# Two graph layers on one core: where the row sums of the attention weights are summed and inverted

## The reference

```
h = relu(layernorm(x))
q, k, v = h Wq' + bq, h Wk' + bk, h Wv' + bv
weight = adj * exp(q k')                     # 256 x 256 per graph
weight = weight / sum(weight, over the keys)
x = x + weight v                             # layer 0
h = relu(layernorm(x))
deg = sum(adj, over j);  agg = (adj h) / max(deg, 1e-6)
x = x + relu([h, agg] W1')                   # layer 1
```

## Time and profile before

| | before |
|---|---|
| median of 3 runs | 2078.81 us (2077.85 to 2078.81) |
| span of the profiled execution, first to last instruction | 2075.8 us |
| what lies around the span (median less span) | 3.0 us |
| TensorE busy | 2033.4 us, 98% |
| VectorE busy | 1420.9 us, 68% |
| GpSimd busy | 1015.8 us, 49% |
| ScalarE busy | 772.6 us, 37% |

### The profile page before, as it was taken

One profiled execution on the slowest core, in us unless ns is written; L12 is line 12 of the kernel. 1 busy time (PEld: TensorE's weight loads), 2 busy tenths in 40 slices (PEclk: granted clock), 3 DMA queues, 4 the chain that ended last, 5 costly groups with the idle time before them and its releaser, 6 DMA issues.

```text
span 2075.8 us, 28517 instructions
## 1 busy us (share of the span) xinstructions
PE 2033.4 (98%) x9852; PEld 1702.4 (82%) x9852; DVE 1420.9 (68%) x2329; ACT 772.6 (37%) x1289; POOL 1015.8 (49%) x958
## 2 busy tenths in 40 slices
PE   8899999999999999999999999999999999999999
PEld 5688888888888888888888888888888888888887
DVE  6877676776667776767767677766677676767654
ACT  3433434333343334343333433344433334333432
POOL 3555553554544555535555445455355554454520
PEclk9999999999999999999999999999999999999999
DMA  5121122212222221222122221212221222212101
GB/s 188 61 76 67 66 76 91 81 51 76 72 85 81 70 72 66 76 91 81 51 72 75 86 81 65 76 66 76 91 81 51 71 76 86 81 60 82 63 29 51
DMA packets 114753, 155.30 MB, mean 75 GB/s; under 512 B 10800, under 2 KB 75312, under 8 KB 114736
## 3 DMA queue, kind: packets, MB, share of 16 engines
q1 hardware_dynamic: 114736, 155.08, 22.0%
HBM read 121.38 MB, written 33.68 MB: 75 GB/s over the span
## 4 chain that ended last, share of the span: by engine, by line
PE 87%; DVE 10%; issue 1%; DMA 0%; SPq 0%; ACT 0%; DVEq 0%; ACTq 0%
PE bank L337 28%; PE bank L339 28%; PE bank L338 28%; DVE hT_l L689 4%; PE bank L345 3%; DVE y L800 1%; DVE x L815 1%; DVE sums L834 1%; DVE h L831 1%; DVE h L730 0%; DMA x_in<-x 0%; DVE sum_inv L836 0%; DVE w_l L175 0%; DVE w L745 0%; DVE v_l L684 0%
## 5 line engine op out<-in xcount | busy, mean ns | idle before, releaser
L292 POOL TENSOR_TENSOR xT<-xT,shared 128x512 f32<-128x512 f32 x248 | 455.5, 1874 | 162.0 <-DMA shared<-norms 162.0
L325 POOL TENSOR_TENSOR at_l<-adjT,at_h 128x1024 fp32r<-128x1024 f32 x32 | 81.4, 2545 | 308.4 <-ACT at_h L675 308.4
L337 PE MATMUL bank<-hT_h,n_h 128*128 128x512 f32 x512 | 204.0, 399 | 23.6 <-DVE x L815 23.1
L269 POOL TENSOR_TENSOR rs<-var_eps,minus_half 128x2 f32<-128x2 f32 x128 | 89.7, 701 | 272.4 <-DVE var_eps L706 272.4
L730 DVE CUSTOM_DVE_ANT_0 h<-h,u_b,bqk 128x512 f32<-128x512 f32 x128 | 215.0, 1731 | 0.0
L535 ACT ACTIVATE h<-x,rs 128x512 f32<-128x512 f32 x124 | 94.1, 807 | 313.5 <-POOL rs L275 313.5
L579 ACT ACTIVATE y<-bank 128x512 f32<-128x512 f32 x128 | 76.7, 599 | 355.6 <-PE bank L339 355.6
L175 POOL TENSOR_TENSOR w_l<-w,w_h 128x512 fp32r<-128x512 f32 x62 | 80.4, 1297 | 255.1 <-ACT w_h L597 255.1
L338 PE MATMUL bank<-hT_l,n_h 128*128 128x512 f32 x512 | 200.3, 391 | 0.0
L339 PE MATMUL bank<-hT_h,n_l 128*128 128x512 f32 x512 | 200.1, 391 | 0.0
L337 PE MATMUL bank<-wv_h,hT_h 128*128 128x512 f32 x512 | 199.2, 389 | 0.0
(11 more groups left out here) (125 smaller groups left out, 4865.9 us busy)
## 6 DMA issues: line engine op xcount, KB each, us to landing
x_in<-x SPq DMA_DIRECT2D x32, 1024.0 KB, 5.3
xT<-x_t SPq DMA_DIRECT2D x62, 512.0 KB, 6.6
out<-x SPq DMA_DIRECT2D x124, 256.0 KB, 2.0
adjT<-adj_t SPq DMA_DIRECT2D x32, 512.0 KB, 3.5
shared<-adj SPq DMA_DIRECT2D x32, 512.0 KB, 4.8
shared<-norms SPq DMA_DIRECT2D x31, 512.0 KB, 3.6
x<-wq SPq DMA_DIRECT2D x4, 256.0 KB, 3.8
xb<-wk SPq DMA_DIRECT2D x4, 256.0 KB, 4.4
```

Source lines behind the costliest of these rows:

```text
L269: pool.tensor_tensor(rs[n][:, 0, tiles], var_eps[n][:, tiles], minus_half[:, :], ALU.pow).then_inc(rstd_done[n], 1)
L292: pool.tensor_tensor(tile, tile, norms[:, k * T:(k + 1) * T, :], (ALU.mult, ALU.add)[k]).then_inc((xT_scaled, xT_shifted)[k], 1)
L325: pool.tensor_tensor(at_l[:, :, :], adjT[:, :, :], at_h[:, :, :].bitcast(F32), ALU.subtract).then_inc(at_split, 1)
L337: pe.matmul(dst, lh, rh, start=first, stop=False)
```

## The change

For a step that has a layer 1 and a following pair (steps 1 to 30), TensorE issues `sums()` after `layer1_products(1)`, and VectorE runs `sum_inverses()` after `layer1_result(1)` and `low_hT(1)`. In step 0 and step 31 both stay where they were. No instruction is added or dropped.

```
--- before.py
+++ after.py
@@ -500,8 +500,10 @@
                 if layer1 and more:
                     for t in range(T):
                         layer1_products(t)
-                if layer0:
-                    if layer1:
+                        if t == 1:
+                            sums()
+                if layer0:
+                    if layer1 and not more:
                         sums()
                     for t in range(T):
                         av(t)
@@ -891,11 +893,14 @@
                     for t in range(T):
                         layer1_result(t)
                         low_hT(i + 1, t)
+                        if t == 1:
+                            sum_inverses()
                 if layer0:
                     if not layer1:
                         for t in range(T - 1):
                             low_hT(1, t)
-                    sum_inverses()
+                    if not (layer1 and more):
+                        sum_inverses()
                     if not layer1:
                         low_hT(1, T - 1)
                     layer0_result(0)
```

## The result

The changed kernel takes 2045.02 us (median of 4 runs, 2044.71 to 2046.76) against 2078.6 us before (a fourth run has joined the three behind 2078.81): a ratio of 0.984, 95% interval 0.983 to 0.986. The forecast was 2047 us with a range of 2043 to 2058.

A forecast was written before the change was run, and what follows sets the result against it. TensorE's stream was taken as the bound, with a stall at step boundaries: 30 boundaries x 1.06 us = 31.8 us off the 2075.8 us span gives 2044.0, plus 3.0 around it makes 2047 us, range 2043 to 2058.

The forecast's parts named there:

- TensorE's stall is the only thing to gain: TensorE, busy 98% of the span: only its waits for the first `layer0_result`, 23.1 us in 31 waits, could yield time.
- 0.91 us of hole per boundary, 30 times: Between a step's last `av` matmul and the next first keys product, TensorE loses 0.91 us; closing this at 30 boundaries.
- the slow return to pace: After the hole, the 48 matmuls of the four keys products take 11.06 us against 10.91 in `z`: 0.15 us per boundary.
- The inverses are hidden at the new place: VectorE behind `low_hT(1)`: the 1.64 us of inverses fit an idle stretch of 2.26 us, 0.6 us to spare, cost 0.
- TensorE's two matmuls cost nothing where they are put: Between `layer1_products(1)` and `layer1_products(2)`: the sums' 0.47 us only delays products 2 and 3; `av(0)` starts as before, net 0.
- 0.03 us to spare at the first keys product: At `kp(0)`: the weight load may start at 1026.30 and is due at 1026.33, so the hole just closes.
- rival 2: First `layer0_result` (L815) still late at the step's end: each 0.1 us costs 3 us, about 2056 us; chance 0.12.
- the hold-up by `at_l`: At the step's end GpSimd's `at_l` holds up VectorE's `low_hT(3)`, 2.88 us against 0.69 alone; expected to stay.
- The back edge of the loop is hidden: TensorE's branch in the loop over steps 2 to 30 was taken to cost 0, with 17 us kept for the range.
- SyncE's 0.56 us: Most that branch, registers and a met wait take on SyncE; rival: TensorE's back edge shows, 2053 to 2064 us, chance 0.13.
- No transfer gets in the way: SyncE: no DMA added or moved; output stores of tiles 2 and 3 and the adjT load shift by 0.47 us.
- what I called the surroundings of the span: Time around the profiled span: the median lay 3.0 us over it (2078.8 against 2075.8), taken as unchanged.

The follow-up runs named there:

- experiment 1: Changed kernel with VectorE's `sum_inverses()` put back behind the last `low_hT`, so only TensorE's sums are moved: 2092.1 us.
- experiment 5: Changed kernel with one small, unused one-column reciprocal on VectorE in front of the first layer 0 result: 2047.5 us.
- experiment 6: Changed kernel with four small, unused one-column reciprocals on VectorE in front of the first layer 0 result: 2051.8 us.
- experiment 9: Changed kernel with the four reciprocals of experiment 6 and with GpSimd's `at_l` waiting for the last low part of hT: 2044.8 us.
- experiment 4: Kernel before the change, sums and inverses at the old place, with GpSimd's `at_l` waiting for the last low part of hT: 2045.3 us.
- Experiments 4 and 10: The `at_l` wait put into the kernel before (experiment 4, 2045.3 us) and into the changed kernel alone (2046.4 us).
- experiment 2: Changed kernel with both sums and inverses one tile later, behind tile 2 (`t == 1` becomes `t == 2`): 2046.7 us.

## Why the prediction was right

- **TensorE's stall is the only thing to gain.** Right: the waits for the first layer 0 result went from 31 to 1, and TensorE's share of the chain from 87 to 97%.
- **0.91 us of hole per boundary, 30 times.** Right. The second term, the slow return to pace, was 0.15 us and measured 0.17 (11.06 - 10.89): I had compared with the 48 matmuls of `z`, which follow shorter ones and have a little slow start of their own. A step fell by 1.08 us, not 1.06.
- **The inverses are hidden at the new place.** Right, with more room than I read: 1.03 us idle instead of 0.6. Against TensorE, the second `low_hT` ends 0.2 us earlier than in the rows of before, the inverses end 1.54 us behind it instead of 1.64, and the third result is released 0.1 us later than forecast. The first of these comes from GpSimd, which holds up the first `low_hT`: its xT tiles now end 14.5 us before the next first keys product (988.75 + 7.79 against 1011.02) where they ended 14.2 us before the moment at which it was due. Why GpSimd is 0.3 us earlier against TensorE was not tried.
- **TensorE's two matmuls cost nothing where they are put.** Right as a sum, and experiment 1 shows the sign of each part: alone they cost 0.47 us a step.
- **0.03 us to spare at the first keys product.** Right: the load starts 0.07 us after the result ends and exactly on pace, and the two doses of experiments 5 and 6 both give 0.03 us. That the sum fell on the good side was in part luck: it adds rows rounded to 0.01 us, and behind tile 2 the same work ends 0.04 us too late. What a miss would cost was put too high in rival 2 (3 us for each 0.1 us, and part of the slow return on top): in experiment 6 a load 0.23 us late costs 0.18 us a step, 5.4 us in 30. The prediction had named the hold-up by `at_l` (2.88 against 0.69 us) but treated it as given, so it missed that the margin hangs on it (experiment 9) and that the stall could be removed without the change (experiment 4).
- **The back edge of the loop is hidden.** Right: the starts are 0.22 to 0.24 us apart across the 30 boundaries in and around the loop, and the steady steps are 62.42 us (one 62.43). Nothing of SyncE's 0.56 us shows on TensorE. The queues that bring instructions again moved 10 and 7 packets, fewer than the 28 back edges. The Trainium skill ("Runtime: NRT & Kernel Launch", "Instruction fetch mechanics") has a stall only for a branch whose target lies outside the fetched pages, and the trace agrees: no stall, and too few packets for a fetch at each back edge.
- **No transfer gets in the way.** Right: in the list of waits no wait for a transfer is longer or more frequent than before, but for a few tenths.
- **The time.** 2047 against 2045.0. Of the 2 us, 1 is in the span (2044.0 against 2043.0): 30 x 0.02 = 0.6 us from the step, and 0.3 us because step 0 ended earlier in this execution (its next first keys product at 74.59 instead of 74.93). The other 1 us is the distance from the span to the median: I took 3.0 us, the median less the span of another execution; the same subtraction now gives 2.0. In every later run the time of an execution is 1.7 to 1.9 us over its own span, so the profiled execution of before was itself some 1 us faster than its median, and what I called the surroundings of the span held that scatter. The gain of the medians, 33.6 us against 31.8 forecast, has the same 1 us in it; that of the spans is 32.8 us.

## What to carry to other kernels

When an engine's queue is late for a consumer by less than the work that stands in front of the late instruction, list every piece of that work, hold-ups by a neighbour included: each piece that, less what its removal delays elsewhere, exceeds the lateness is a cure by itself (here 1.64 - 0.47 = 1.17 us and 2.2 us, against a weight load 1.14 us late). Work that depends on old data belongs in an idle stretch earlier in the queue, but its producer must move too, and the move of the producer alone can cost time. After the cure, compare the moment of release with the moment at which the weight load is due, not with the matmul's: here the time was won with 0.03 us to spare.

## What the runs showed of the hardware

- **What GpSimd holds up.** Beside a running GpSimd instruction with two SBUF inputs, VectorE's instructions with two SBUF inputs wait (L691 2.12 to 2.89 us instead of 0.69, L807 1.17 instead of 0.69), and the held L691 ends 0.54 to 0.56 us after GpSimd's instruction does. Those with one input in PSUM (layer 0 result 0.75) or a single SBUF input (reduction 0.69, statistics 0.70) run at full speed. Experiments 4 and 10 put them side by side.
- **A late weight load costs a little less than its lateness.** Against the changed kernel's step of 62.42 us, a load of the first keys product that comes 0.04 us late costs 0.03 us (experiment 5), 0.23 costs 0.18 (experiment 6), 1.14 costs 1.08 (before: 1027.47 - 1026.10 - 0.23), and 1.64 costs 1.56 (experiment 1, whose load before it starts at 1032.49). So the hole and the slow return to pace are one price, and it can be read from the load alone.
- **Executions differ by 1 to 2 us before the steady part.** The window of 30 to 35 us of the changed kernel and of experiment 2, and the first keys product of step 1 in each (the number behind GpSimd's busy time is the granted clock):

```profile
30.00:35.00 5.00, 5.00 (x22) 4.07 (x22) 2.30 (x5) 1.36 (x2) 0.00 (x0) 0.97 0.96 332
```

```profile
74.59 0.51 PE L337 MATMUL bank<-hT_h,n_h 128*128 128x512 f32 x1 [0.29 <-DVE x L817]
```

```profile
30.00:35.00 5.00, 5.00 (x14) 3.87 (x14) 3.14 (x5) 0.88 (x2) 0.00 (x0) 0.58 0.78 265
```

```profile
77.05 0.47 PE L337 MATMUL bank<-hT_h,n_h 128*128 128x512 f32 x1 [1.00 <-DVE x L817]
```

TensorE is busy for only 3.4 and 3.3 of the 5 us from 20 to 25 us, in the setup's transposes, and its granted clock, full before, then falls: in the next 5 us it is 0.69 and 0.73, a mix of the 1.2 and 2.4 GHz levels. In the window shown the first kernel is back at the 2.4 GHz level for nearly all of it (0.97), the second mostly at 1.2 (0.58), and step 1 begins 2.5 us later, with the same code up to there. The twelve traces, which all have that code, fall in line: where the granted clock of this window is 0.92 to 1.00 (eight of them) step 1 begins at 74.19 to 74.94, and where it is 0.58 to 0.79 (four) at 75.89 to 77.05. After that the changed kernel's steps repeat to 0.01 us. What decides how soon the clock is back is not shown, and each kernel has one trace, so that the runs of one kernel scatter for this reason is argued and not shown; their scatter is of this size, which is why the steady step was used for small effects.
